# Attention of an adaLN transformer block on one NeuronCore: the loop over key/value pairs written out

## What is computed

```
s = einsum(q, k) / 8                       # rotated q and k, head width 64
a = s**2 * exp(G[t] - G[s])                # for s <= t, else 0; G: running sum of log gates
num = a @ v                                # the sum over a cancels in the norm that follows
m = max over s of a                        # per row, it enters the guard 1e-6
y = layernorm(num / ...) * ln_w
```

## Time and profile before

| | us |
|---|---|
| median of 3 runs (2408.23 to 2412.22) | 2410.38 |
| the profiled execution's own time | 2411.28 |
| its span, first to last instruction | 2409.6 |
| of it, attention, from PE's first score to the last one's reduction | 357.4 to 1561.6 |
| PE busy | 2167.4 (90%) |
| DVE busy | 1874.8 (78%) |
| ACT busy | 1368.3 (57%) |
| POOL busy | 824.7 (34%) |

### The profile page before, as it was taken

The page is one execution under the profiler, slowest core; times in us unless marked ns, Lnnn a source line. Parts: engine busy times, 40 slices in busy tenths (PEclk is TensorE's granted clock), DMA queues, the critical chain, the costliest instruction groups (busy, mean ns, idle before and its releaser), DMA issues. The chain is left out here.

```text
span 2409.6 us, 46005 instructions
## 1 busy us (share of the span) xinstructions
PE 2167.4 (90%) x12429; PEld 1316.2 (55%) x12429; DVE 1874.8 (78%) x2813; ACT 1368.3 (57%) x2415; POOL 824.7 (34%) x793
## 2 busy tenths in 40 slices
PE   7888869999999999999999999779963799999994
PEld 5666643333333333333333333369952799999994
DVE  6888858878788787887878878767868777767673
ACT  4555547666666666676666666434420465656562
POOL 4777741101001110010110001036644565656564
PEclk9999989999999999999999999979985799999997
DMA  5444442220222211222102222034441243434344
GB/s 165 127 122 125 125 135 71 79 69 21 76 74 74 75 40 52 74 74 74 58 34 74 79 75 74 25 113 132 131 152 59 75 85 78 84 80 82 72 91 103
DMA packets 192862, 205.44 MB, mean 85 GB/s; under 512 B 44408, under 2 KB 169536, under 8 KB 185728
## 3 DMA queue, kind: packets, MB, share of 16 engines
q1 hardware_dynamic: 160096, 156.26, 21.0%
q0 software_dynamic: 15840, 22.29, 5.9%
q10 hardware_dynamic: 16768, 25.17, 3.3%
HBM read 132.64 MB, written 75.24 MB: 86 GB/s over the span
## 5 line engine op out<-in xcount | busy, mean ns | idle before, releaser
L891 ACT ACTIVATE att_sb_a<-att_ps_s,att_sb_fg,att_sb_f 128x1024 f32<-128x1024 f32 x384 | 458.9, 1203 | 351.9 <-PE att_ps_s L1044 351.9
L946 DVE TENSOR_TENSOR att_sb_acc<-att_sb_acc,att_sb_a 128x768 f32<-128x768 f32 (+3 forms) x532 | 533.2, 1030 | 36.9 <-ACT att_sb_a L891 33.9
L837 POOL TENSOR_SCALAR_AFFINE_SELECT att_sb_dec<-att_sb_dec 128x128 f32<-128x128 f32 x260 | 123.5, 475 | 1066.4 <-ACT att_sb_dec L880 1064.3
L963 DVE SCALAR_TENSOR_TENSOR att_sb_a<-att_ps_s,att_sb_dec 128x1024 f32<-128x1024 f32 (+3 forms) x260 | 212.3, 822 | 124.2 <-PE att_ps_s L1044 81.8
L1044 PE MATMUL att_ps_s<-first_sb_q,first_sb_k 64*128 64x512 f32 (+3 forms) x1288 | 297.4, 568 | 9.1 <-DVE att_sb_q L928 9.1
L1044 PE MATMUL att_ps_s<-att_sb_q,att_sb_k 64*128 64x512 f32 (+3 forms) x1296 | 292.1, 556 | 0.0
L1828 DVE TENSOR_TENSOR ffn_sb_h_lo<-ffn_sb_h,ffn_sb_h_hi 128x256 fp32r<-128x256 f32 x320 | 212.6, 702 | 35.3 <-ACT ffn_sb_h_hi L1716 34.0
L1723 ACT ACTIVATE ffn_sb_h<-ffn_ps_p,ffn_sb_b_cols 128x256 f32<-128x256 f32 x320 | 151.7, 477 | 136.8 <-PE ffn_ps_p L1914 134.5
L895 ACT ACTIVATE att_sb_a<-att_sb_a 128x1024 f32<-128x1024 f32 (+3 forms) x260 | 189.0, 727 | 56.2 <-DVE att_sb_a L963 56.2
L1044 PEld LDWEIGHTS att_ps_s<-first_sb_q,first_sb_k 64*128 64x128 f32 x1288 | 108.7, 189 | 200.9 <-issue 122.3
L1044 PEld LDWEIGHTS att_ps_s<-att_sb_q,att_sb_k 64*128 64x128 f32 x1296 | 107.9, 186 | 194.7 <-issue 123.9
(11 more groups left out here) (252 smaller groups left out, 4136.9 us busy)
## 6 DMA issues: line engine op xcount, KB each, us to landing
ffn_sb_raw<-L_ffn_W ACTq DMA_DIRECT2D x36, 512.0 KB, 3.5
att_sb_hb<-half_log SPq DMA_DIRECT2D x17, 1024.0 KB, 11.1
close_sb_nT<-num_rows SPq DMA_DIRECT2D x34, 512.0 KB, 4.0
num_rows<-att_sb_num SPq DMA_DIRECT2D x65, 256.0 KB, 2.1
q_rows<-proj_sb_rT SPq DMA_DIRECT2D x64, 256.0 KB, 2.3
first_sb_q<-q_rows SPq DMA_DIRECT2D x9, 1024.0 KB, 5.1
first_sb_k<-k_rows SPq DMA_DIRECT2D x18, 512.0 KB, 8.6
v_cent<-proj_sb_vt SPq DMA_DIRECT2D x32, 256.0 KB, 2.4
```

Source lines behind the costliest of these rows:

```text
L891: nc.scalar.activation(a[:, g, :, :], s_ps[slot(at[st])][:, :, :], ACT.Square, scale=f[:, r.p, i - 1, s:s + 1], bias=fg[:, r.p, i - 1, s:s ...
L946: nc.vector.tensor_tensor(x[:, :, c:TB], x[:, :, c:TB], a[:, a_slot(st), :, c:TB], ALU.max).then_inc(max_done, 1)
L963: nc.vector.scalar_tensor_tensor(a[:, a_slot(st), :, j * P:TB], s_ps[slot(r.order["s"].index(st))][:, :, j * P:TB], GUARD, dec[:, dec_slot ...
```

## The change

All 16 pairs are written out, on every engine, with no loop. A place is now a number that runs through all pairs (44 per pair; carried steps get the place of the following pair's turn), each kind of job has one order over all pairs (`Order`), and a wait is for the constant rank of a job in it. So the score slots (rank modulo 3), the buffers for squares (rank modulo 8) and the others are counted through all pairs, due times are no longer cut at the turn's end, and decays whose due time is negative in a turn move into the turn before. Gone are the carried steps of the pair that does not exist, the zeroing and its waits, the credits, the scores for a pair 16, the second load of pair 0, the separate ending, and `apart` in this stage. SP loads pair 1 at once behind the first `hb`, and pair q + 2 right behind the store of block 3 of pair q. The numbers of matmuls, squares and maxima per pair are the same.

```
-AHEAD = 3
-FIRST = ("o1 d3 o1 d3 x0 o1 d3 o1 d3 "
+PATTERN = ("o1 d3 o1 d3 x0 o1 d3 o1 d3 "
            "o2 o2 d1 o2 d1 o2 x3 o2 d1 o2 d1 o2 o2 "
            "o3 d2 o3 d2 o3 x1 o3 d2 o3 d2 o3 o3 d0 o3 d0 x2 o3 o3 d0 o3 d0 o3")
-LAST = "o1 d3 o1 d3 x0 d3 d3 x3"
-CARRIED = {("diag", 3), ("max", 3), ("max", 0)}
+CARRIED = ("d3", "x3", "x0")
+def attention_places():
...
+    for body in range(PAIRS + 1):
+        for n, (carried, kind, i, s) in enumerate(pattern):
+            q = body - carried
+            if 0 <= q < PAIRS:
+                place[q, kind, i, s] = body * N + n
+    return N, place
+class Order:
+    def __init__(self, places):
+        self.ops = sorted(places, key=lambda op: (places[op], op))
+        self.rank = {op: k for k, op in enumerate(self.ops)}
+    def count(self, op):
+        return self.rank[op] + 1
...
-    def values_at(st):
-        d = at[st] + (2.5 if st[0] == "off" else 5.5)
-        return min(d if int(d) % 2 else d + 1, N + AHEAD - 0.7)
+    def values_at(op):
+        d = place[op] + (2.5 if op[1] == "off" else 5.5)
+        return d if int(d) % 2 else d + 1
...
-        return min(at[st] + 4.8, N + AHEAD)
+        return place[op] + 4.8
...
-    pe_todo = [(at[st], "s", st) for st in steps[AHEAD:]] + [(N + at[st], "next", st) for st in steps[:AHEAD]]
+    pe_todo = [(place[op], "s", op) for op in place] + [(values_at(op), "av", op) for op in offs + diags]
...
-    def slot(n):
-        return n % SR
+    def slot(op):
+        return s_order.rank[op] % SR
...
         @block.sync
...
-            load_logs(0, 0)
-            sp.wait_ge(zero_done, 2)
-            with sp.Fori(0, PAIRS // 2) as it:
-                for p in range(2):
-                    r = turn(it * 2 + p, p)
-                    sp.wait_ge(av_done, ready(r.nth("av", last_own[3])))
-                    apart(sp, keep)
...
+            load_logs(0)
+            load(1)
+            for n, (q, i) in enumerate(total_order):
+                sp.wait_ge(num_done, n + 1)
+                sp.dma_start(num_rows[q, :, i * TB:(i + 1) * TB], num[:, n % 2, :]).then_inc(num_st[n % 2], 16)
+                if i == 3 and q + 2 < PAIRS:
+                    load(q + 2)
...
         @block.gpsimd
-            pool.sem_inc(dec_done, CREDIT)
-            nc.gpsimd.memset(k_sb[1][:, :], 0.0)
-            nc.gpsimd.memset(v_sb[1][:, :, :], 0.0)
-            nc.gpsimd.memset(hb[1][:, :], 0.0)
-            nc.gpsimd.memset(nh[:, 1, :], 0.0).then_inc(zero_done, 1)
...
         @block.scalar
-            act.wait_ge(zero_done, 2)
-            act.wait_ge(pair_in[0], LOADS)
-            factors(0, 0)
...
-            with act.Fori(0, PAIRS // 2) as it:
+            arrived(act, 0)
+            factors(0)
             for _, what, op in act_todo:
...
         @block.vector
-            nc.vector.memset(part[:, :, :], 0.0)
-            for i in range(NB):
-                nc.vector.memset(acc[:, i, :, :], 0.0)
-            nc.vector.memset(q_sb[1][:, :], 0.0).then_inc(zero_done, 1)
-            dve.wait_ge(zero_done, 2)
...
-            with dve.Fori(0, PAIRS // 2) as it:
-                for p in range(2):
-                    r = turn(it * 2 + p, p)
-                    for _, what, op in dve_todo:
...
         @block.tensor
-            pe.wait_ge(zero_done, 2)
-            pe.wait_ge(pair_in[0], LOADS)
-            for n in range(AHEAD):
-                scores(turn(0, 0), steps[n], n)
-            with pe.Fori(0, PAIRS // 2) as it:
...
-            for n in range(AHEAD, len(tail)):
-                user = tail[n - SR]
-                if user[0] != "off":
-                    wait_slot(end, user, 0)
-                scores(end, tail[n], n)
-                last_values(n - AHEAD + 1)
+            for _, what, op in pe_todo:
+                if what == "s":
+                    scores(op)
+                else:
+                    values(op)
```

More of the change, by code:

```diff
@@ L651 @@
[L651 to L669, removed]
+PATTERN = ("o1 d3 o1 d3 x0 o1 d3 o1 d3 "
+           "o2 o2 d1 o2 d1 o2 x3 o2 d1 o2 d1 o2 o2 "
+           "o3 d2 o3 d2 o3 x1 o3 d2 o3 d2 o3 o3 d0 o3 d0 x2 o3 o3 d0 o3 d0 o3")
@@ L704, in attend @@
[L704 to L721, removed]
@@ new lines, in attend @@
+    act_todo += [(place[op] - 5, "dec", op) for op in diags]
+    act_todo += [(place[q, "off", i, 0] + 0.5, "et", (q, i)) for q, i in blocks]
+    act_todo += [(q * N + N * 0.85, "factors", (q + 1,)) for q in range(PAIRS - 1)]
+    dve_todo = [(max_at(op), "max", op) for op in offs + diags]
+    dve_todo += [(place[op] + 0.3, "own", op) for op in diags]
+    dve_todo += [(place[op] + 0.6, "row", op) for op in maxes]
+    dve_todo += [(max_at(last_off(q, i)) + 0.01, "scale", (q, i)) for q, i in blocks]
@@ new lines, in attend, with slot_user, a_slot, a_user @@
+    dve_todo += [(values_at(last_off(q, i)) + 1.2, "part", (q, i)) for q, i in blocks]
+    dve_todo += [(values_at(last_own(q, i)) + 1.2, "total", (q, i)) for q, i in owns]
+    pe_todo.sort(), act_todo.sort(), dve_todo.sort()
+    def slot(op):
+        return s_order.rank[op] % SR
+    def slot_user(op):
+        k = s_order.rank[op] - SR
+        return s_order.ops[k] if k >= 0 else None
+    def a_slot(op):
+        return slots.rank[op] % A
+    def a_user(op):
+        k = slots.rank[op] - A
+        return slots.ops[k] if k >= 0 else None
@@ L915, in _ @@
-            for _, what, op in act_todo:
-                if what == "dec" and op in ending["dec"]:
-                    decay(end, op)
-                elif what == "sq" and op in ending["sq"]:
-                    square(end, op)
+                    wait(act, av_done, av_order, a_user(op))
+                    wait(act, max_done, max_order, a_user(op))
+                    act.wait_ge(s_done, s_order.count(op))
+                    nc.scalar.activation(x, s_ps[slot(op)][:, :, :], ACT.Square,
+                                         scale=f[:, p, i - 1, s:s + 1], bias=fg[:, p, i - 1, s:s + 1]).then_inc(sq_done, 1)
+                else:
+                    act.wait_ge(own_done, own_order.count(op))
+                    nc.scalar.activation(x[:, :, c:TB], x[:, :, c:TB], ACT.Square).then_inc(sq_done, 1)
@@ L1008, in _ @@
-            for _, what, op in dve_todo:
-                if what == "max" and op in ending["max"]:
-                    maximum(end, op)
-                elif what == "own" and op in ending["own"]:
-                    own_scores(end, op)
-                elif what == "row" and op in ending["row"]:
-                    rows(end, op)
-                elif what == "total" and op == 3:
-                    total(end, op)
+                    dve.wait_ge(part_done, part_order.count((q, i)))
+                    nc.vector.tensor_tensor(num[:, n % 2, :], part[:, et_order.rank[q, i] % 2, :], own_ps[:, :], ALU.add).then_inc(num_done, 1)
@@ new lines, in rows @@
+            def rows(op):
+                q, _, i, _ = op
+                dve.wait_ge(s_done, s_order.count(op))
+                nc.vector.tensor_reduce(keep.row_max[:, q, i * ST:(i + 1) * ST, :].rearrange("p c h -> p h c"),
+                                        s_ps[slot(op)][:, :, :].rearrange("p h (c k) -> p h c k", k=P), AX.X, ALU.max).then_inc(row_done, 1)
+            for _, what, op in dve_todo:
+                if what == "max":
+                    maximum(op)
+                elif what == "own":
+                    own_scores(op)
+                elif what == "row":
+                    rows(op)
+                elif what == "scale":
+                    scale(*op)
+                elif what == "part":
+                    before_own(*op)
+                else:
+                    total(*op)
```

368 lines of the change are left out of this document (142 added, 226 removed).

## The result

The changed kernel takes **2336.81 us** in the median (2335.93 to 2340.65, four runs), the kernel before 2409.93 (2408.23 to 2412.22, four runs). The ratio is 0.9694 with a 95% interval of 0.968 to 0.9709: 3.1% faster, 73.1 us. The forecast was 2346 with a range of 2326 to 2370. The profiled execution of the changed kernel took 2336.56 us, with a span of 2334.8 against 2409.6, so the two traces have 74.8 us to account for.

The account below looks back on a forecast made before the run. PE was taken to set the time inside a turn, with a gap of about 5 us at each branch back, where DVE is late. Gains of 48.9 + 9.5 + 6.0 = 64.4 us gave 2346 us, range 2326 to 2370.

Parts of the forecast that it names:

- (1): Attention loop's seven branches back: writing them out saves 7.0 us each, 5.1 idle and the rest slower matmuls, 48.9 us.
- (2): Start of the attention stage: no zeroing and no steps of a pair that does not exist, 9.5 us gained.
- (4): Waits on constants and counting through all pairs: taken at 0, bounds 24 us gain and 22 us loss.
- the spared steps: At the start, PE's transposes, last diagonal scores and value products of the pair that does not exist: 5.2 us.
- The unknown: At the start, pair 1's load behind hb might slow it: start 6.5 us later, gain 3; taken as no cost.
- (3): End of the attention stage: no pair 16 score steps, and 4.0 of DVE's 4.26 us idle won, 6 us.
- The bound named, 8: Upper bound in us of the gain at the stage's end, if PE's idle time before x3 shrinks as well.
- rival B: Waits in the turns did cost: turns shrink by up to 1.5 us, 2322 us; chance 0.08.
- The bound of 24 us: Upper bound of gain from constant waits: about 20 lone score steps a turn at 0.075 us, 1.5 a turn.
- Rival A: New lags at pair boundaries, DVE or ACT late for x0 or d3: loses up to 22, 2368 us; chance 0.14.
- (5): SP's later loads, fewer loads and semaphore increments, and POOL's work lie beside other work: nothing gained or lost.
- Rival C: Written-out code must be fetched for every pair, stalling engines: 112 us on top, 2458 us, slower; chance 0.04.

## Why the prediction was right, and which step was off

**(1) The branches: right, and shown.** 48.9 us were forecast, 49.4 are gone from the trace, and 48.6 go when the loops alone are written out. The reading behind it holds too. Of five branches only DVE's matters (DVE alone wins 47.4 us, the others nothing), and its cost splits as said, into the wait for its next instruction and PE's slower clock behind it. In the kernel before, the stretch with the transposes x0 behind the first gap has a granted clock of 0.50 (columns as above):

```profile
511.50:513.50 2.00, 1.97 (x10) 1.65 (x10) 1.89 (x2) 0.99 (x1) 0.00 (x0) 0.50 0.00 0
```

In the changed kernel PEclk is 1.00 in both stretches shown, and the transposes take 1.06 to 1.09 where they took 1.96.

That the wait is the fetching of code was a reading in the prediction, and the runs carry it further. The wait is "<-issue", stays when every other engine goes straight on, and goes when the code of DVE alone is written out. And code does come in while it lasts. The queues for instructions in the kernel before, from 505.26 to 510.17 us, which is DVE's first gap:

```profile
q14 instruction: 2, 0.02, 1.3%
```

Two such packets lie in each of the seven gaps (4.65 to 4.91 us), in each of the seven when only DVE keeps its loop, and in each of the three with a body of four (4.70 to 4.79 us). With DVE's loop alone written out the queue brings none from 505 to 511 us, and 24 in the stage in place of 51. That DVE waits for these two packets, and does not stand still beside them, is the one step that stays a reading. The Trainium skill's 108 ns for a compare-and-branch (Advanced Engine Details and Errata, section Control Flow Timing) describes none of the gaps.

**(2) The start: 9.7 in place of 9.5.** The stretch gained 10.2 us, of which 0.5 is the boundary that belongs to (4). The near hit is in part luck, since the step's parts moved against each other. `hb` was taken to land after 4.6 us, as in the kernel before, and took 5.6; so the first value product came 14.65 - 9.63 = 5.0 us earlier and not 5.9. From there to x0 of pair 0 another 5.2 were won, 4.7 without the boundary, against a net 3.6 in the working: if the spared steps were rightly sized at 5.2, only 0.5 of the 1.6 set against them for the clock and for bubbles showed. The unknown, that pair 1's load (3.5 MB with its own `hb`, not 2.5) could slow the first `hb`, was rightly taken as no cost: the experiment with the load held back shows `hb` no faster.

**(3) The end: 7.8 in place of 6.0.** The mechanism was right: DVE's idle time before x0 fell from 4.26 to 0.38 us, and the score steps of pair 16 are gone. I took 4.0 of the idle time and two score steps; the trace gives 4.7 up to x0 and 3.2 behind it. The bound named, 8, held, and for the reason given: PE's idle time before x3 shrank from 3.73 to 0.33 us.

**(4) Waits on constants, counting through: taken at nothing, and it was 7.5 us over the 15 boundaries.** This is the step that failed in size. It priced two different things together. The waits' forms are indeed worth nothing (70.76 us a turn either way). But the due times that are no longer cut were only looked at for a new lag. What they did was to move the last value step of a turn behind a score step, so that PE changes twice less between scores and values, at 0.18 us each; another 0.14 us went ahead of x0. The earlier trace rows had the sign of it in sight, a lone step of 1.13 us against 1.99 for two, and I put that down to the waits, as rival B, and not to the change of kind. (The bound of 24 us worked out from it does not stand: a turn has 6 lone score steps, not 20, and by the starts of the rows a lone one takes 1.06 us against 0.96.) So the time came out 9 us under the forecast, in B's direction but for another reason. Rival A, new lags at the boundaries, is wrong: turns are shorter, with no idle time of PE in the stretches above.

**(5) SP and POOL: nothing, as forecast.** The loads of `hb` now land after 14.2 us in the median in place of 11.1, and nobody waits for one: in the stage PE has no wait for a DMA but the first.

**Rival C, code fetched again, is wrong.** Fetching did rise, as it had to. The queues of instructions in the attention stage of the changed kernel, 355 to 1490 us, against 6 (q8) and 51 (q14) packets before:

```profile
q8 instruction: 44, 0.72, 0.3%
q14 instruction: 33, 0.27, 0.1%
```

Eight of these packets came from 641 to 782 us, and PE was busy for 141.00 of 141.00 us. The Trainium skill, Runtime: NRT & Kernel Launch, section Instruction fetch mechanics, says that straight code is brought in ahead and that a jump out of the resident blocks has to wait. The runs agree on both: no "<-issue" gap of the old kind in straight code, and 4.65 to 4.91 us on DVE at each jump back.

The sum by steps: 49.4 + 9.7 + 7.8 + 7.5 = 74.4 against 64.4 forecast; the stages around add 0.4 more.

**What stays open.** Why a change of kind costs 0.16 to 0.20 us was not settled. The two kinds differ in rows (64 for scores, 128 for values), in the width of the weights and in where they write, and no run changed one of these alone. The 0.14 us ahead of x0 in the kernel before were not isolated either; that they go with the counting of score slots through all pairs is only argued.

## What to carry to other kernels

A loop on an engine that others wait for at the branch can cost far more than the branch: look for a gap "<-issue" that recurs once a body, find the engine whose own row has it, and write out that engine's loop first; the others may keep theirs. Where PE is busy all the time, count how often it changes between kinds of matmul and gather steps of one kind, then follow the new wait (here the bank of a sum) and move the step that frees it. A loop's cut in due times or slots also fixes the order at its edge, so an unrolled loop should be priced for its new order as well as for the branch.

## What the runs showed of the hardware that was not expected

- PE pays 0.16 to 0.20 us for each change between score steps (64 rows) and value steps (128 rows), although it counts as busy all the time. If each of the 48 changes in a turn costs that, it is some 120 us of the kernel (16 x 48 x 0.16, an estimate).
- The wait at a branch back depends on the engine and on the size of the body: DVE 4.65 to 4.91 us with a body of two turns or of four; PE nothing with two turns and 0.74 to 1.02 us with four; ACT 1.2 to 1.5 us with four. In each of DVE's waits two packets of instructions, of 8 KB each, come in.
- A load of 1 MB that is first in its queue landed after 5.6 us with 3.5 MB issued right behind it and after 5.85 alone; it varies from 4.6 to 5.9 us between the traces, with or without loads behind it.
